# One transformer block over eight images: PSUM banks by kind of work, an order of steps for every engine, and three images in one period

## The reference, cut to what matters

```python
h = h + attention(layernorm(h), Wq, bq, Wk, bk, Wv, bv, Wo, bo)
h = h + ffn(layernorm(h), ...)
```

## Time and profile before

| | us |
|---|---|
| median of 3 runs | 1160.15 |
| the profiled execution, its own time | 1158.63 |
| its span, first to last instruction | 1156.8 |
| TensorE busy (matmuls) | 1030.7 |
| VectorE busy | 756.9 |
| ScalarE busy | 626.8 |
| GpSimd busy | 387.0 |
| mean granted TensorE clock | 0.946 |

### The profile page before, as it was taken

One profiled execution on the slowest core, in us unless ns is written; L12 is line 12 of the kernel. 1 busy time (PEld: TensorE's weight loads), 2 busy tenths in 40 slices (PEclk: granted clock), 3 DMA queues, 4 the chain that ended last, 5 costly groups with the idle time before them and its releaser, 6 DMA issues.

```text
span 1156.8 us, 16622 instructions
## 1 busy us (share of the span) xinstructions
PE 1030.7 (89%) x5632; PEld 694.0 (60%) x5632; DVE 756.9 (65%) x2118; ACT 626.8 (54%) x1395; POOL 387.0 (33%) x514
## 2 busy tenths in 40 slices
PE   2489988999889988999889998899979998899997
PEld 1355566656675556755666556665667555675575
DVE  3378548874578647785387854887467863778444
ACT  1226825567345763567454683556834665456754
POOL 5321424314343133412353142531334223441243
PEclk9969988999889997999889998999988999899999
DMA  3430041202240040400404004220314004040000
GB/s 97 67 48 1 6 52 42 38 2 30 26 63 17 1 56 10 61 10 1 56 10 69 2 2 56 42 37 2 43 14 66 14 2 55 10 66 1 1 1 18
DMA packets 28547, 34.60 MB, mean 30 GB/s; under 512 B 5402, under 2 KB 15552, under 8 KB 28336
## 3 DMA queue, kind: packets, MB, share of 16 engines
q1 hardware_dynamic: 28464, 33.55, 18.6%
HBM read 3.61 MB, written 4.19 MB: 7 GB/s over the span
## 4 chain that ended last, share of the span: by engine, by line
PE 74%; DVE 7%; DMA 6%; SPq 5%; ACT 4%; issue 2%; POOL 2%; DVEq 0%; POOLq 0%; ACTq 0%
PE bank L517 15%; PE bank L536 12%; PE pair L488 9%; DMA k_stack<-qk_h 5%; PE pair L659 5%; PE bank L488 5%; SPq L361 5%; PE pair L661 5%; PE pair L660 5%; ACT pt L972 3%; PE pair L419 2%; PE pair L420 2%; PE pair L421 2%; PE bank L639 2%; PE bank L431 1%
## 5 line engine op out<-in xcount | busy, mean ns | idle before, releaser
L972 ACT ACTIVATE pt<-bank 128x512 f32<-128x512 f32 (+3 forms) x768 | 346.7, 493 | 195.7 <-PE bank L517 188.2
L744 DVE CUSTOM_DVE_ANT_0 pair<-pair,causal 128x640 f32<-128x640 f32 (+3 forms) x256 | 257.0, 1048 | 34.7 <-PE pair L488 33.7
L517 PE MATMUL bank<-q_stack,k_stack 128*128 128x512 f32 (+3 forms) x768 | 264.4, 395 | 9.7 <-ACT pt L972 7.3
L517 PEld LDWEIGHTS bank<-q_stack,k_stack 128*128 128x128 f32 x768 | 135.4, 189 | 162.8 <-ACT pt L972 127.5
L1116 POOL TENSOR_SCALAR_AFFINE_SELECT pt<-pt 128x512 f32<-128x512 f32 x128 | 81.4, 636 | 352.6 <-ACT pt L972 352.6
L536 PE MATMUL bank<-pt,v 128*32 128x512 f32 (+3 forms) x1536 | 166.1, 505 | 2.5 <-ACT pt L972 2.5
L744 DVE CUSTOM_DVE_ANT_0 bank<-bank,causal 128x128 f32<-128x128 f32 (+3 forms) x256 | 121.7, 509 | 66.8 <-PE bank L488 66.6
L488 PE MATMUL pair<-k_stack,q_stack 112*128 112x512 f32 (+3 forms) x512 | 147.2, 377 | 7.1 <-issue 6.2
L488 PE MATMUL bank<-k_stack,q_stack 112*128 112x128 f32 (+3 forms) x256 | 86.9, 411 | 37.9 <-DMA k_stack<-qk_h 31.0
L488 PEld LDWEIGHTS pair<-k_stack,q_stack 112*128 112x128 f32 x512 | 87.0, 192 | 42.8 <-DVE mx L744 26.8
L659 PE MATMUL pair<-wex_h,hid_h 128*128 128x512 f32 x256 | 106.9, 418 | 0.7 <-POOL hid_l L1139 0.4
(11 more groups left out here) (142 smaller groups left out, 1498.4 us busy)
## 6 DMA issues: line engine op xcount, KB each, us to landing
q_stack<-qk_h SPq DMA_DIRECT2D x64, 128.0 KB, 3.9
k_stack<-qk_h SPq DMA_DIRECT2D x64, 128.0 KB, 6.4
q_stack<-qk_l SPq DMA_DIRECT2D x32, 128.0 KB, 5.1
k_stack<-qk_l SPq DMA_DIRECT2D x32, 128.0 KB, 6.7
out<-h SPq DMA_DIRECT2D x16, 256.0 KB, 2.3
pt<-w_expert SPq DMA_DIRECT2D x1, 1024.0 KB
x_sb<-x_t SPq DMA_DIRECT2D x8, 116.0 KB
pos_sb<-pos SPq DMA_DIRECT2D x1, 512.0 KB
```

The source lines that it names most:

```text
L517: nc.tensor.matmul((b4, b5)[p % 2][:, c0:HALF], k_stack[:, hd // 2, kt * P:(kt + 1) * P], q_stack[:, half, hd, c0:HALF], start=True, stop= ...
L744: nc.vector.tensor_tensor_reduce(src, src, causal[:, S - n:S], 1.0, -3.0e38, ALU.add, ALU.max, mx[:, col:col + 1]).then_inc(s_taken, 1)
L972: nc.scalar.activation(pt[:, k % PT_SLOTS, j, q0:HALF], (b4, b5)[p % 2][:, q0:HALF], ACT.Exp, scale=0.25).then_inc(exp_done, 1)
```

## The change

The diff rewrites most functions, so it is told first, and then shown where code says it better.

- **Banks** (all single): two for scores, two for `prob`, one for `weigh`, two for the forward steps (the `a` product or expert group 0 goes to the first, the `b` product or group 1 to the second), and one, `m_bank`, for all 30 front, behind and turn steps of a period. Each m step waits for `m_taken` of the step before it in TensorE's order.
- **Scores**: no instruction is wider than 512 keys. For units 2 and 3 the 32 far tiles (keys of half 0) get a plain maximum (`tensor_reduce` into `mx_far`), the 32 diagonal ones the masked one; `maximum` joins the two.
- **Moved instructions**: the rests `zt_l` and `qk_l` are made on VectorE straight from PSUM (before: GpSimd from SBUF), and ScalarE's plain copy of q and k goes away.
- **Buffers**: those of a half hold one half; `h` has 5 slots of half an image, `v` two images, `k_stack` three places (half 0 of two images, one of half 1); hidden and selected values have buffers of their own. Front and behind share none.
- **Order**: one string per engine. A period holds steps of three images: behind and forward of half 1 of image n; scores of units 2 and 3, all of `prob`, `weigh`, and behind and forward of half 0 of image n+1; front and scores of units 0 and 1 of image n+2. It runs for n = -2 to 7, and steps of images that don't exist fall out.
- **SP**: queries and keys are moved by steps of their own. Queries of half 1 wait until the last `prob` matmul of the image before has been made, and so do keys of half 1. What stands behind them in SP's order waits too.

```diff
+def image_of(st):
+    if st[0] in ("emb", "turn1", "ztl", "q", "k", "v", "queries", "keys"):
+        return 2
+    if st[0] == "score":
+        return 2 if st[1] < UNIT_S[1] else 1
+    if st[0] == "turn":
+        return 2 if st[1] < 2 else 1
+    if st[0] in ("prob", "weigh", "take"):
+        return 1
+    half = (st[1] // HT if st[0] in ("in", "hid", "expert", "combine") else st[1])
+    return 1 - half
...
+    middle = (behind(1) + [("shared", 1), ("turn", 2)] + behind(0) + [("turn", 3)] + front(0) + [("shared", 0)] + front(1) +
+              [("turn", 0), ("turn", 1)])
...
+    "pe": (
+        "mssppspsmsppsmssmppsspwpsswppsmsspsmcspsfppsfssfsmwsfmsppsmsffpsfppfwmsppfsspfspwpswssfspsmspspf"
+        "ssfwmsppsfspspwspswfspswmpfsmppssmssppsmpsspwwspsfspmpspssmmmpsmpswpcpfmpfmwmppffppwpfpffpcpmmfw"
+        "ppfmfcppmpwppfpmwppmdpfppmfwpwppssfspssdmdspmswsspmscsppwcsppsmppswspspmsspfspspmwpdspscfppsswps"
+        "spfppssfsswswsfwcm"
+    ),
...
+PROGRAM = {}
+for engine in ("pe", "dve", "act", "pool", "sp"):
+    PROGRAM[engine] = [(n + image_of(st), st) for n in range(-2, B) for st in period(WEAVE[engine], streams())
+                       if 0 <= n + image_of(st) < B]
...
-        bank = [ctx.enter_context(nc.psum_tensor(f"bank{n}", [P, HALF], F32)) for n in (4, 5, 6, 7)]
-        pair = [ctx.enter_context(nc.psum_tensor(f"pair{n}", [P, 2 * HALF], F32)) for n in range(2)]
-        b4, b5, b6, b7 = bank
+        s_bank = [bank(f"bank_s{n}") for n in range(2)]
+        p_bank = [bank(f"bank_p{n}") for n in range(2)]
+        w_bank = bank("bank_w")
+        f_bank = [bank(f"bank_f{n}") for n in range(2)]
+        m_bank = bank("bank_m")
...
+            def queries(i, half):
+                sp.wait_ge(m_taken, after(i, "q", half))
+                if i:
+                    sp.wait_ge(st_ready, ((i - 1) * NP_ + HALF_P[half]) * G4)
+                for n, part in enumerate((qk_h, qk_h, qk_l)):
+                    for odd in range(2):
...
+            def keys(i, half):
+                sp.wait_ge(m_taken, after(i, "k", half))
+                if half and i:
+                    sp.wait_ge(st_ready, i * NP_ * G4)
+                elif i > 1:
+                    sp.wait_ge(st_ready, (i - 1) * NP_ * G4)
...
+            def m_free(i, st):
+                if before(i, *st):
+                    pe.wait_ge(m_taken, before(i, *st))
...
+            def score(i, s):
+                u, t, j, diag = SCORES[s]
...
+                if s == UNIT_S0[0] or s == UNIT_S0[2]:
+                    pe.wait_ge(q_in[half], (i + 1) * 96)
+                if s == UNIT_S0[0] or s == UNIT_S0[2] + ROWS:
+                    pe.wait_ge(k_in[half], (i + 1) * 96)
+                if i * NS + s >= 2:
+                    pe.wait_ge(s_taken, i * NS + s - 1)
...
+            def split_turned(i, half):
+                n = half_no(i, half)
+                dve.wait_ge(zt_made, n + 1)
+                nc.vector.tensor_tensor(zt_l[:], m_bank[:], words(zt_h[:]), ALU.subtract).then_inc(m_taken, 1)
+
+            def split_projected(i, st):
+                w, half = "qk".index(st[0]), st[1]
+                dve.wait_ge(qkh_made, half_no(i, half) * 2 + w + 1)
+                nc.vector.scalar_tensor_tensor(qk_l[:, w, :], m_bank[:], (bq_sb, bk_sb)[w][:, 0:1], words(qk_h[:, w, :]),
+                                               ALU.add, ALU.subtract).then_inc(m_taken, 1)
...
+                if not diag:
+                    nc.vector.tensor_reduce(mx_far[:, col:col + 1], s_bank[s % 2][:], AX.X, ALU.max).then_inc(s_taken, 1)
+                    return
...
+            def maximum(i, u):
+                if u >= 2:
+                    dve.wait_ge(s_taken, i * NS + UNIT_S[u])
+                    mine = slice(u * ROWS, (u + 1) * ROWS)
+                    nc.vector.tensor_tensor(mx[:, mine], mx[:, mine], mx_far[:, mine], ALU.max).then_inc(mx_made, 1)
```

More of the change, by code:

```diff
@@ L121, in streams @@
             weighing.append(("take", UNIT_LAST.index(k)))
-    middle, forward = [], []
-    for half in range(2):
-        middle += [("to", half), ("ant", half), ("oproj", half), ("emb", half), ("z2t", half), ("gates", half),
-                   ("route", half, 0), ("turn1", half), ("route", half, 1), ("route", half, 2), ("q", half), ("k", half)]
-        middle += [("v", 1), ("counts", 1), ("shared", 1)] if half else [("counts", 0), ("shared", 0), ("v", 0)]
-        forward += [("in", q, ab) for q in range(4 * half, 4 * half + 4) for ab in range(2)]
-        forward += [("expert", t, g) for t in range(HT * half, HT * half + HT) for g in range(GROUPS)]
@@ new lines, in behind @@
+    def behind(half):
+        return [("to", half, 0), ("to", half, 1), ("ant", half), ("oproj", half), ("z2t", half), ("gates", half),
+                ("route", half, 0), ("route", half, 1), ("route", half, 2), ("counts", half)]
+    middle = (behind(1) + [("shared", 1), ("turn", 2)] + behind(0) + [("turn", 3)] + front(0) + [("shared", 0)] + front(1) +
+              [("turn", 0), ("turn", 1)])
+    forward, combine = [], []
+    for half in (1, 0):
+        for q in range(4 * half, 4 * half + 4):
+            forward += [("in", q, 0), ("in", q, 1)] + ([("hid", q - 1)] if q % 4 in (1, 2) else [])
+        forward += [("expert", t, g) for t in range(HT * half, HT * half + HT) for g in range(GROUPS)]
+        combine += [("combine", t) for t in range(HT * half, HT * half + HT)]
@@ L147, in period, with before, after, half_before @@
     return [next(left[name]) for name in weave]
-PERIOD = period(WEAVE, streams())
-FIRST = sorted((st for st in PERIOD if of_next_image(st)),
-               key=lambda st: (3 if st[0] == "turn" or st[0] == "score" and st[1] >= 6 else
-                               2 if st in (("q", 1), ("k", 1), ("v", 1)) else 1 if st[0] == "score" else 0))
-LAST_WEAVE = (
-    "sppssppssppswspsppsppspwsppsppwsppwsppswppsppwsspspwppspsppspwpspspwpswppssppwpssppwppssppwppsps"
-    "ppwppsmppwppmppwppppwppmppwwpppwpppmpwpmppmwppffmppwppfpfpfpwmpfppfpfpmwppwppmwwfmfmcfmfffccfmfm"
-    "cfmfffffmffmfffmfmccffffcc"
-)
-LAST = period(LAST_WEAVE, {name: [st for st in stream if not of_next_image(st)] for name, stream in streams().items()})
+PROGRAM = {}
+for engine in ("pe", "dve", "act", "pool", "sp"):
+    PROGRAM[engine] = [(n + image_of(st), st) for n in range(-2, B) for st in period(WEAVE[engine], streams())
+                       if 0 <= n + image_of(st) < B]
+MISC = ("emb", "turn1", "q", "k", "v", "to", "ant", "oproj", "z2t", "gates", "counts", "shared", "turn")
+MISC_BEFORE = {step: n for n, step in enumerate(step for step in PROGRAM["pe"] if step[1][0] in MISC)}
+def before(i, *st):
+    return MISC_BEFORE[i, st]
+def after(i, *st):
+    return MISC_BEFORE[i, st] + 1
+def half_before(i, half):
+    return (i, 0) if half else (i - 1, 1)
 def build(nc, x_t, tok_w, pos, wq, wk, wv, wo, bq, bk, bv, bo, ln_s, ln_b, w_in, w_shared, w_expert, w_bias,
@@ L347, in _, with ones @@
             sp.wait_ge(stacks_zeroed, 3)
[L348 to L356 removed]
+            def ones(place, many):
+                for n in range(HEADS // 2):
+                    sp.dma_start(words(k_stack[SHIFT:P, n, place:place + many, :]),
+                                 words(minus1[:, 0:many, :])).then_inc(ones_in, 16)
@@ L674, in stage @@
                     weigh(i, st[1])
-                elif of_next_image(st):
-                    front(i, st[0], st[1])
-                elif st[0] in ("in", "counts", "shared", "expert"):
-                    forward(i, st, more)
-                elif st[0] != "combine":
-                    post(i, st, more)
-            def image(i):
-                for st in PERIOD:
-                    stage(i + of_next_image(st), st)
-            pe.wait_ge(w_in0, 2 * 16)
-            stage(0, FIRST[0])
```

1163 lines of the change are left out of this document (546 added, 617 removed).

## The result

The changed kernel took **1126.28 us** (median of 4 runs, 1125.81 to 1126.66), against 1157.36 (4 runs) of the kernel before beside it: a ratio of 0.9747, 95% interval 0.9721 to 0.9773. The forecast was 1120, with a range of 1078 to 1172. The profiled execution's own time was 1126.66, its span 1124.9, its mean granted clock 0.972 (before: 0.946). The kernel before, run again beside each batch of the experiments, took 1155.95 to 1157.98 us, so medians of different batches compare to within some 2 us.

A forecast was written before the change was run, and what follows sets the result against it. VectorE was to bound stretch A, TensorE with m-bank rounds the rest: 68 + 58 + 2.5, said 129 us a period; 343 us of ends + 6 x 129 = 1117 of span, 1120 us as median, range 1078 to 1172.

The forecast's parts named there:

- A: Stretch of a period from `to` of half 1 to gates of half 0, with the scores of units 2 and 3: 68 us.
- TensorE's work and the m bank: Per period: matmuls 116.3 us, plus 7.3 us where 13 of 30 single-bank rounds outlast the work between them: 123.6.
- The walk: Through TensorE's string between m steps, taking the larger of round and work: 123.6 us a period, 13 of 30 rounds binding.
- B: Rest of the period, no scores at first, then those of units 0 and 1: 58.0 us.
- VectorE as the bound of A: VectorE's 63 us of work in A, at most 0.938 busy, needs at least 67 us; 68 taken.
- The bubble: At the period's start TensorE waits for half 1's queries: 8 us of DMA against 5.7 of work, 2.5 us a period.
- rival on the stacks: Queries of half 1 land as late as the stacks before: bubble 8 us, period 134.5, 1161 us; chance 0.12.
- The clock: Forecast: it holds. Rival: falls at the boundary cost 3.4 us each, one or two a period, 1145 to 1171 us; chance 0.06.
- The ends: Deeper pipeline costs outside the six full periods: head 68, period -1 110, last two 114 and 51; 343 us against 332.
- The splits: Six subtractions a period moved from GpSimd to VectorE at 0.69 us: 4.1 us more VectorE work, lower `qk_l` latency.
- The slower rival: Each of 30 m-bank rounds meets one more 0.69 us instruction on its taker: period 144.3, 1235 us; chance 0.14.
- No stalls: Rival: the orders fit the chip and the period is 123.6, 1080 us; chance 0.12.

The follow-up runs named there:

- the run with short far maxima: Far maxima read 128 of their 512 columns, against the best kernel: 1108.16 us.
- the best kernel: Queries moved by head group, those of half 0's second group behind its keys, against the changed kernel: 1101.06 us, ratio 0.9509 to the kernel before.
- ten steps late: Ten of VectorE's m steps a period one place later in its own order, against the changed kernel: 1215.50 us, ratio 1.0488.
- one order: TensorE's order of steps given to VectorE, ScalarE and GpSimd too, SP's kept, against the changed kernel: 1365.65 us, ratio 1.1807.

## Why the prediction was right, and where its steps were off

**The outcome** was right, 1126 against 1120, partly because errors cancel: the time and the period fit, several of the signs that the prediction named for itself do not (the clock is 0.972 where it wanted 0.98, VectorE 83% busy in A where it wanted 90, the wait 1.6 us where it wanted 2 to 3, the turn's wait 0.8 where it wanted under 0.5), and one of its signs of being wrong, "a clock of 0.5 after each boundary", came true.

**TensorE's work and the m bank.** The walk (116.3 of work and 7.3 of rounds, 123.6; of it A 65.6 and B 58.0) has its measure in the kernel without a boundary wait or clock fall: 126.4, A 62.7 and B 63.7. The sum is 2.3% off, its halves by -2.9 and +5.7. Its two terms are off as well, in opposite directions. In the period from 430.4 to 556.8 TensorE stands idle 4.7 us, and the distances from one matmul to the next, without that, add up to 121.7. The excess over 116.3 is in the price of the wide ones among scores and probs: in this order 512 columns cost 0.32 us in a score and 0.28 in a prob, not the 0.23 that the prediction read off (waits too short to show as idle may be in it; with VectorE relieved the score still costs 0.31). Scores and probs took 24.0 and 22.4 us, where it had 20.3 each (by its own prices 20.2).

**VectorE as the bound of A** is the step that failed. "63 in A" is 54.2 (B 42.9, where I had 40), 83% of A and not 94%, and taking 94 us off it made nothing faster, twice. The far maximum was right (0.684 us for 0.69), the whole 97.1 for 103.4. About 3 us of the difference is small instructions that got shorter (below). So A's 68 came near the measured 65.6 for the wrong reason: 1.6 us of A was the wait for the queries and up to 1.7 the clock. The sum had 70.5 for A and the bubble, which lies in A, and 58.0 for B; measured are 65.6 and 63.6. That the two errors cancel is luck.

**The bubble** was the right mechanism at 2.5 us; 1.6 was measured at `q_stack`, behind 0.8 at the turn. (The prediction's own terms give 7.8 - 5.7 = 2.1, and its rival on the stacks took off 6.4 where this sum took 5.7.) From the first issue to the first score 8.8 us passed, where I had 8. The rival on the stacks had the cause, bytes on the wires, and five times the size.

**The clock.** "The clock should hold: no bubble of more than 3 us is left" is the second step that failed. It fell at every boundary, and in half of the periods once more: windows of 5 us over the six periods add up to 37 us at 1.2 GHz, so up to 3.1 us a period. With the wait that covers the distance from 126.4 to 130.0. The prediction gave that 0.06, on the ground that falls had followed only idle stretches of about 3 us. Here TensorE was busy 1.56 of 4 us before the fall, and in the run with short far maxima 2.74 of 4; the longest single idle at a steady boundary was 1.6 us. So this rival's condition came true. It counted 3.4 us of loss for a fall; here seven of the nine falls of the six periods lasted 3.4 us at 1.2 GHz, up to 1.7 us of loss each, and the 3.1 us a period is still near its lower price. Its time of 1145 was missed because it stood on a period of 129 that held VectorE's bound: that the forecast's number came true although the clock fell is luck. The Trainium skill ("TensorE: Matmul & The Clock Gate", A second HAM failure mode: psum-queue depth-cycling) says of a bf16 kernel that short idles between groups of matmuls, from cycling through PSUM, can make the clock go back and forth. I had set it aside; these runs agree that short idles are enough, also in float32: at the boundary one of 0.8 us from the m bank and one of 1.6 from a DMA, in the run with short far maxima two of 0.5 us from the m bank and one of 0.9 behind an exp.

**The ends.** Head 66.4 (68), period -1 114.8 (110), last two pieces 161.6 (165). Period -1 held 6.8 us at 1.2 GHz around 80, which I had not counted.

**The splits** were called nearly free, and are worth 34 to 72 us; that they hardly matter was wrong.

**The slower rival** was underpriced: it had 144.3 us a period with all thirty rounds in its condition, and ten are enough for 142.9. Why it did not come to pass is argued, not shown: of the 24 m steps that VectorE takes part in, 17 stand between the same scores in its string as in TensorE's, one stands ahead of scores that TensorE has before it, and six stand behind one or two scores more. **No stalls** (1080) needs 123.6; the best kernel stops at 126.4.

So the gain of 31 us is: six periods shorter by 7.1 us each on the mean (137.5 to 130.4), minus 10.7 at the ends. A period before held 15.1 us at 1.2 GHz on the mean and one after 6.2, so if each cost its half, 4.4 of the 7.1 is clock. No run took away the banks, the narrower scores or the three images by themselves, so what each of them gave stays open; what is shown is that the change lives on its orders and on the place of the splits. With the order of the queries mended, the same idea brings 56 us.

## What to carry to other kernels

When streams share banks with one buffer each, the order of every taker is the design: check each engine's string against the producer's, step for step, DMA queues too, before counting anyone's load. Price a wait on TensorE with the clock fall behind it, read from the granted clock of the windows after it; a wait of 1.6 us came with 2 us more. When a removed wait brings nothing, look for the same DMAs further down the same queue.

## What the runs showed of the hardware

Small VectorE instructions took a third to a half of their time after the change, with the same shapes: the mean of the wsel product fell from 542 to 174 ns, that of cmp_eq from 454 to 218. Source view of the product, before and after (shortest, median and longest in ns):

```profile
L851 DVE TENSOR_TENSOR wsel<-topp,trec x16: 174/177/1041, 137.7 to 1138.0; 128x16 f32<-128x16 f32 x16
```

```profile
L814 DVE TENSOR_TENSOR wsel<-topp,trec x16: 174/174/178, 120.0 to 1104.2; 128x16 f32<-128x16 f32 x16
```

So the mean hides two kinds. The timeline of the kernel before shows what stood beside a long one:

```profile
467.37 1.28 POOL L1104 TENSOR_TENSOR qk_l<-ot,qk_h 128x512 fp32r<-128x512 f32 x1 [0.68 <-ACT qk_h L956]
```

```profile
467.63 1.04 DVE L851 TENSOR_TENSOR wsel<-topp,trec 128x16 f32<-128x16 f32 x1
```

The product ends at 468.67, where GpSimd's subtraction does (468.65). In the kernel before, the seven products that overlap an instruction of GpSimd took 1014 ns on the mean and the other nine 175; of cmp_eq eight took 689 and eight 218. In the changed kernel none of either overlaps one. It is not so of every instruction: the reduce `emax` took 170 ns with and without GpSimd beside it. With the splits back on GpSimd, wsel and cmp_eq stayed short (174 and 218 ns), and they met no instruction of GpSimd there either: the stretching goes with the meeting, not with GpSimd's load.

The second surprise is how much of every difference here can have gone through the clock: 20 us at 1.2 GHz in the best kernel, 63 in the changed one, 125 before, 144 with ten steps late, 226 with one order, for the same matmuls.
